# Graph attention kernel: softmax pieces moved to even steps, weighted tiles around the sums, an early SiLU table, scores behind alpha's input

## What is computed

```python
h = relu(layernorm(x))
message = (h @ w_src + b_src)[src] + (h @ w_dst)[dst]
rad = silu(silu(edge_scalars @ w1 + b1) @ w2 + b2) @ w3 + b3
message = message * edge_weight * rad
msg_h = (message @ w_sep + b_sep).reshape(E, 8, 32)      # 8 heads: 16 for alpha, 16 values
a = msg_h[:, :, :16]
alpha = 0.6 * a + 0.4 * a * (2 * sigmoid(a) - 1)
score = einsum('ehk,ahk->eh', alpha, alpha_dot)
att = segment_softmax(score, dst)
out = x + segment_sum(msg_h[:, :, 16:] * att, dst).reshape(N, 128) @ w_proj + b_proj
```

## Time and profile before

| | |
|---|---|
| median of 3 runs | 5095.57 us (5094.09 to 5096.37) |
| profiled execution | 5094.63 us, span of its instructions 5092.7 us |
| TensorE (PE) busy | 4832.5 us, 95% of the span |
| VectorE (DVE) busy | 3848.3 us, 76% |
| ScalarE (ACT) busy | 2626.1 us, 52% |
| GpSimd (POOL) busy | 3618.4 us, 71% |
| mean granted TensorE clock | 0.973 |
| L1251 table loads | 52, 1283 ns each |
| L1245 table loads | 51, 1283 ns each |

### The profile page before, as it was taken

One profiled execution on the slowest core, in us unless ns is written; L12 is line 12 of the kernel. 1 busy time (PEld: TensorE's weight loads), 2 busy tenths in 40 slices (PEclk: granted clock), 3 DMA queues, 4 the chain that ended last, 5 costly groups with the idle time before them and its releaser, 6 DMA issues. The chain is left out here.

```text
span 5092.7 us, 92871 instructions
## 1 busy us (share of the span) xinstructions
PE 4832.5 (95%) x28995; PEld 3449.1 (68%) x28995; DVE 3848.3 (76%) x6981; ACT 2626.1 (52%) x3939; POOL 3618.4 (71%) x3491
## 2 busy tenths in 40 slices
PE   3599999999999999999999999999999999999975
PEld 2456777777776777777677777777777777777764
DVE  6547777777777777777777777777777777777777
ACT  2455555555555555555555555555555555555511
POOL 2377777777777777777777777777777777777716
PEclk9799999999999999999999999999999999999975
DMA  6666666666666666666666666766666666666625
GB/s 188 191 202 200 211 200 212 204 206 207 202 211 202 211 202 206 206 202 211 202 209 205 205 208 199 213 203 207 205 206 208 201 209 205 207 206 206 207 64 157
DMA packets 889681, 1019.24 MB, mean 200 GB/s; under 512 B 161780, under 2 KB 778008, under 8 KB 888863
## 3 DMA queue, kind: packets, MB, share of 16 engines
q1 hardware_dynamic: 758843, 774.32, 47.3%
q0 software_dynamic: 108784, 223.44, 17.6%
q10 hardware_dynamic: 21556, 15.50, 1.2%
HBM read 863.59 MB, written 152.34 MB: 199 GB/s over the span
## 5 line engine op out<-in xcount | busy, mean ns | idle before, releaser
L1056 POOL DMA_INDIRECT gath<-msg_src,idx x3328 | 3475.5, 1044 | 1176.5 <-issue 1030.8
L1245 ACT ACTIVATE sil<-a_ps,ba 128x512 f32<-128x512 f32 x832 | 571.7, 687 | 1648.1 <-PE a_ps L1367 1580.7
L1375 PEld LDWEIGHTS v_ps<-wv,msgT 128*128 128x128 f32 x6656 | 835.5, 191 | 526.2 <-issue 526.2
L1305 PEld LDWEIGHTS rad_ps<-wval,hot 128*128 128x128 f32 x6656 | 911.5, 194 | 79.0 <-DVE wval L1147 35.6
L1305 PE MATMUL rad_ps<-wval,hot 128*128 128x136 f32 x6656 | 929.3, 284 | 32.5 <-DVE wval L1147 31.3
L1375 PE MATMUL v_ps<-wv,msgT 128*128 128x128 f32 x6656 | 924.1, 282 | 0.0
L1367 PE MATMUL a_ps<-msgT,wa 128*128 128x512 f32 x1664 | 890.7, 617 | 30.9 <-DVE msgT L1178 30.9
L1178 DVE TENSOR_TENSOR msgT<-xT_ps,rads 128x512 f32<-128x512 f32 x832 | 572.4, 688 | 354.1 <-PE xT_ps L1348 307.9
L1197 DVE SCALAR_TENSOR_TENSOR sil<-a_ps,sil 128x512 f32<-128x512 f32 x832 | 567.4, 682 | 354.2 <-ACT sil L1245 351.6
L1294 PE MATMUL xT_ps<-hotT,win 128*128 128x256 f32 x3328 | 730.4, 341 | 0.0
L1230 ACT ACTIVATE vals<-v_ps 128x512 f32<-128x512 f32 x832 | 493.2, 593 | 340.4 <-PE v_ps L1375 319.0
(11 more groups left out here) (234 smaller groups left out, 4147.9 us busy)
## 6 DMA issues: line engine op xcount, KB each, us to landing
rows_bc<-edge_rows SPq DMA_DIRECT2D x416, 768.0 KB
win<-msg_dst SPq DMA_DIRECT2D x1664, 128.0 KB
sums<-run SPq DMA_DIRECT2D x416, 272.0 KB
attr<-in_edge_attr_t SPq DMA_DIRECT2D x1664, 32.0 KB
gath<-msg_src,idx POOLq DMA_INDIRECT x3328
msg_dst<-dst_parts SPq DMA_DIRECT2D x98, 128.0 KB, 2.2
pen_g<-pen_rows SPq DMA_DIRECT2D x208, 32.1 KB
mask_g<-mask_rows SPq DMA_DIRECT2D x208, 32.0 KB
```

The lines of the kernel that those rows point to most:

```text
L1056: pool.indirect_dma_start(gath[:, u, s], None, msg_src, bass.IndirectOffsetOnAxis(ap=idx[:, j // 8, at:at + 1], axis=0)).then_inc(s_gath[u ...
L1245: act.activation(sil[:, j % 8], a_ps[:, :], ACT.Silu, bias=ba[:, :]).then_inc(s_sil, 1)
L1305: last = pe.matmul(rad_ps[:, j % 2, AW * i:AW * (i + 1)], lhsT=hot[:, j % 4, s], rhs=wval[:, j % 4, s].rearrange("p h k -> p (h k)"), star ...
L1375: last = pe.matmul(v_ps[:, s * P:(s + 1) * P], lhsT=msgT[:, q, s * P:(s + 1) * P], rhs=wv[:, :], start=True, stop=True)
```

## The change

- VectorE: the piece of j = 1 moves to step 0, that of j = 5 joins j = 4, that of j = 9 joins j = 8; no piece is left at the end of an odd step. In step 14 the factor comes behind the marks instead of ahead of them.
- VectorE: `weigh` does one tile; in odd steps one tile is weighted ahead of `accumulate` and one behind it.
- ScalarE: behind the exponentials of step 11 stands a SiLU of one column (`spare`), whose result nobody uses.
- TensorE: `scores` comes behind alpha's input instead of ahead of it, and in step 12 therefore behind the transposes of the weights too.

```diff
@@ vector: soft @@
-                    if j == 1:
+                    if j == 0:
                         dve.wait_ge(s_sc, 4 * n + 4)
...
                         dve.tensor_scalar(ends[:, 0:G], sel[:, :], fwd[:, TE - 1:TE], None, ALU.mult).then_inc(s_soft, 1)
-                    elif j == 5:
                         dve.wait_ge(s_soft, k + 4)
...
                         dve.tensor_copy(carry[:, 0:1], carry[:, G:G + 1]).then_inc(s_soft, 1)
-                    elif j == 9:
                         dve.wait_ge(s_soft, k + 14)
@@ vector: weigh @@
-                    for n in range(2):
-                        at = 32 * ((j + n) % 4) + H * (j // 4)
-                        last = dve.tensor_tensor(wval[:, u + n], vals[:, slot + n],
-                                                 wT[:, :, at:at + H].unsqueeze(3).broadcast_to((P, SUB, H, HV)), ALU.mult)
-                    last.then_inc(s_wv, 1)
+                    at = 32 * (j % 4) + H * (j // 4)
+                    product = dve.tensor_tensor(wval[:, u], vals[:, slot], wT[:, :, at:at + H].unsqueeze(3).broadcast_to((P, SUB, H, HV)), ALU.mult)
+                    if j % 2:
+                        product.then_inc(s_wv, 1)
@@ vector: step @@
-                    if group(g - 1) and j == 14:
-                        soft(g - 1, j)
                     if j % 2 == 0:
                         if there(t + 2 - LAG):
                             mark(*later(g, j, 2 - LAG))
+                        if group(g - 1) and j == 14:
+                            soft(g - 1, j)
                         if there(t - LAG):
                             accumulate(*later(g, j, -LAG))
                         if group(g - 1) and j != 14:
                             soft(g - 1, j)
                     else:
+                        if there(t + 1 - LAG):
+                            weigh(*later(g, j, 1 - LAG))
                         if there(t - LAG):
                             accumulate(*later(g, j, -LAG))
-                        if there(t + 1 - LAG):
-                            weigh(*later(g, j, 1 - LAG))
+                        if there(t + 2 - LAG):
+                            weigh(*later(g, j, 2 - LAG))
                         if there(t + 1):
                             scale_rad(*later(g, j, 1))
...
-                    if j % 2 and group(g - 1):
-                        soft(g - 1, j)
@@ scalar: step @@
                         act.activation(shifted[:, :], shifted[:, :], ACT.Exp)
                         act.activation(drop[:, :], drop[:, :], ACT.Exp).then_inc(s_exp, 1)
+                        act.activation(spare[:, :], row_below[:, :], ACT.Silu)
@@ tensor: step @@
                     if group(g - 1) and j in (6, 8, 14):
                         soft(g - 1, j)
-                    if j % 4 == 0 and there(t - 1):
-                        scores(g if j else g - 1, j // 4 - 1 if j else 3)
                     if group(g - 1) and j == 12:
                         soft(g - 1, j)
                     if there(t):
                         pe.wait_ge(s_msg, t + 1)
                         pe.matmul(a_ps[:, :], lhsT=wa[:, :], rhs=msgT[:, q], start=True, stop=True).then_inc(s_a, 1)
+                    if j % 4 == 0 and there(t - 1):
+                        scores(g if j else g - 1, j // 4 - 1 if j else 3)
+                    if there(t):
                         if q and there(t + 1):
```

More of the change, by code:

```diff
@@ L887, in gnn_kernel @@
             row_below = tb("row_below", [P, 1])
+            spare = tb("spare", [P, 1])
             rads = tb("rads", [P, 4, TE])
```

## The result

The changed kernel took 5114.73 us (5111.15 to 5117.6, 7 runs) beside 5096.37 us for the kernel before (5094.09 to 5097.15, 7 runs). The ratio is 1.0036, 95% interval 1.0024 to 1.0047: slower by 18 us, 0.4%. 5102 was forecast, with a range of 5084 to 5128.

What follows compares the result with a forecast made beforehand. TensorE, busy 177.71 of 178.50 us, was taken as the bound. Per group -0.65 - 0.15 - 0.14 + 0.12 + 1.02 = +0.20, fifty times +10, start +3, end -6: total +7, 5102 us, range 5084 to 5128.

Steps and rivals of the forecast that it cites:

- the second rival: Odd steps: the first weighted tile on VectorE makes the sums' addition late; 5122 us, at 0.1 beyond the margin 5142; chance 0.09.
- Step 12, the deciding term: The early table load delays the copy of step 11's values, so TensorE's weight transposes start late: +1.02 us per group.
- Step 10 and step 2: Softmax pieces leaving odd steps no longer delay `msgT` on VectorE: -0.65 us in step 10, -0.15 in step 2.
- Steps 0 and 4: Scores behind alpha's input shorten TensorE's list from sums to z2, 3.79 against 3.86 us: -0.07 each.
- step 8: Small products come first; alpha's exposed weight load moves ahead and the values meet the mode change: +0.12 us.
- The first weighted tile: Odd steps: one tile weighted ahead of the sums fits VectorE's wait with 0.11 us margin; 0, up to +0.1 each.
- The start: 30 steps without sums: scores fill no gap, step 12 pays about 1.9, steps 2, 6 and 10 gain; +3 us.
- The end: 30 steps with sums only: one weighted tile fewer in the chain, 0.64 off some 14 pairs; -6 us.
- The early table that costs nothing: Rival: step 12 gives -0.17 instead of +1.02 us, so 5042 us; chance 0.08.
- The rival by which a switch costs more than its load: Each table switch keeps ScalarE empty another 1.28 us, making step 12's copy later: 5166 us; chance 0.02.

Runs made afterwards that it cites:

- c1: The changed kernel without the added one-column SiLU: 5050.2 us, ratio 0.9910 to the kernel before.
- c4: The kernel before with only the one-column SiLU added behind the exponentials: 5098.87 us beside 5094.82, ratio 1.0008.
- c3: The kernel before with only the softmax pieces of steps 1, 5 and 9 moved into steps 0, 4 and 8: 5051.74 us, ratio 0.9914.
- b4: The changed kernel without the added SiLU, both weighted tiles ahead of the sums in the stream: 6212.7 us against 6199.14, disturbed chip.
- b3: The kernel before with only scores moved behind alpha's input: 6306.19 us against 6199.14, ratio 1.0169, disturbed chip.
- b2: The kernel before with only one weighted tile on each side of the sums: 6169.64 us against 6199.14, ratio 0.995, disturbed chip.
- c2: The changed kernel with scores behind alpha's input only in step 12 and the added SiLU behind the copy of step 11's values: 5038.42 us, ratio 0.9887.
- a2: The kernel before with only the one-column SiLU added behind the exponentials, on a disturbed chip: 6212.47 us against 6212.66, ratio 1.0017.

## Why the prediction was right, and what it missed

The mechanism that decided was right, and so was its price. That the number held owes something to a wide range and to luck. 5114.73 lies just outside the forecast's own range of 5090 to 5114; the 5084 to 5128 took it in because it had been widened for the second rival, which didn't come true. "Within 0.2%", up to 5106, was given 0.52 and didn't hold; what came had 0.21. In the stream the group grew by 0.49, 25 us in all, where 0 to +20 was given. That range was narrower than its own terms, whose ends add up to 0 and +36 even without the odd steps. And of the 15 us by which the stream missed, the end, which gained 5 more than forecast, hid a third.

**Step 12, the deciding term.** Forecast +1.02 and 1.2 us late; measured +1.09 and 1.16. The table load ahead of the copy, behind an order in which scores no longer cover it, is shown from both sides: taking the load away gives 64 us (c1), and the load under the old order costs 4 (c4).

**Step 10 and step 2.** Forecast -0.65 and -0.15; measured -0.66 and -0.15, and c3 has them alone. The exposed weight load that I took at 0.10 was 0.10: alpha's input now takes 0.86, not 0.96.

**Steps 0 and 4.** Forecast -0.07 each, measured 0.00. The step that failed is "0.93 + 0.95 + 0.99 + 0.92 = 3.79", in its last term: the 0.92 of the values behind the radial product was taken up to the destination product, which starts earlier behind the values than z2 does. Ahead of z2 the values take 0.99. The same term makes step 8 +0.20 instead of +0.12 (by the forecast's own terms +0.13, since 2.97 - 2.84) and adds 0.07 in step 12. In the four steps together that is 0.29 us, all by which the group (+0.49) missed the sum (+0.20): 15 us in the stream.

**The first weighted tile.** Forecast 0, measured 0 in the odd steps. Its rival's price was right as well: 0.52 us beyond the margin made each odd step longer by 0.50 (b4).

**The start.** Forecast +3, measured +5.2. Scores steps lost 0.68 instead of 0.5 to 0.6 (5.83 against 5.15), and step 12 lost 3.69 instead of 1.9: behind the idle of 2 us alpha's input and scores ran at the lower clock, 1.6 us longer than at the full one.

**The end.** Forecast -6, measured -11.0. The weighted tiles give 8 to 9 us of it (b3 to b2, c3 to c2), near 14 x 0.64. What I had step 4's and step 10's pieces take back isn't seen: c3 has them moved and took 90.68, b3 has not and took 90.73. The other 2 to 3 us come with the higher clock, which I hadn't in the sum, and b3 and c3 have it without the weighted tiles. So it need not be a gain of the change; whether the shorter waits raise the clock as well wasn't tried by itself.

**The rivals.** The early table that costs nothing would have given 5042. c1 (5050, the table removed) and c2 (5038, at another place) show what that is worth; in the kernel as changed, load, SiLU and the way back cost 1.16 us beyond the 0.5 of slack. The rival by which a switch costs more than its load falls: L1249's exponential starts at 2553.93, 0.01 behind the load's end, and the SiLU L1251 as close behind its own. The Trainium skill (ScalarE: Activation LUTs, What ACT_TABLE_LOAD costs) has 1283 ns for the load, which every load here took, and a drain of about 1380 ns for a switch, which no row here shows.

The median came 13 us above the forecast, the profiled execution 14.6: +15 in the stream, +2 in the start, -5 in the end and +2 ahead of the stream.

## What to carry to other kernels

Where the busiest engine runs an ordered list, price each move by start to start distances, and take the distance of a pair only for the same pair: the time of an operation depends on what stands ahead of it and behind it. Before an operation is moved later, look whom it covered: here scores of 1 us hid a copy that has 0.5 us of slack without them, and a table load of 1.28 us was put ahead of that copy. A table load belongs behind whatever another engine waits for; take such a bundle of edits apart, since one part of this one was worth 43 us and another cost 64.

## What the runs showed of the hardware

A change between the full array and narrow tiles costs in both directions and by neighbour: 0.09 us behind the sums, and behind scores the values take 0.99 instead of 0.89. Over the list of steps 0 and 4 the two cancel, 3.87 us in either order. One idle stretch of TensorE of 2 us was followed by 1.2 GHz (granted clock 0.62 over 3 us), and c1, without that stretch, has no such dip; 50 stretches of about 1.2 us were not followed by one. The length of a single idle doesn't decide it: in the stream of the disturbed a2, 71 of TensorE's 135 idles of 2 to 3 us had 1.2 GHz somewhere in the 5 us behind their end, and 7 of 113 of 1 to 1.5 us. And a disturbed chip gives other verdicts: the pieces were worth 43 us on a quiet one and nothing that could be measured (0.9991) on the same chip while it was disturbed, when the order of the scores alone cost 1.7%.
